# Own orders for the filling steps of a transformer block, with GpSimd's set-up work and the weight load split

## What is computed

```python
x = x + tanh(g_xattn) * xattn(layernorm(x), ctx)         # q from x, k and v from the context, softmax, Wo
x = x + tanh(g_ffn)  * block(layernorm(x))
# block: h = rms(x) * n1
#        q, k = rms per head of h @ wq.T, h @ wk.T; v = h @ wv.T; causal softmax; @ wo.T (first 32 columns zeroed)
#        xf = rms(x + ao) * n2;  gates = top 2 of softmax(xf @ gate_w.T), renormalised
#        o0, o2, o3: gelu networks;  o1: silu(..) * (..);  out = x + sum gates * o  (first 32 columns of the sum zeroed)
```

## Time and profile before

| | us |
|---|---|
| median of 3 runs | 1200.54 (1198.05 to 1200.64) |
| the profiled execution | 1201.37 |
| its span | 1199.6 |
| PE busy | 1030.4 (86%) |
| DVE busy | 828.7 (69%) |
| ACT busy | 740.2 (62%) |
| POOL busy | 346.7 (29%) |

### The profile page before, as it was taken

How to read it: one execution, slowest core, us unless ns; L and a number is a source line. 1 busy time by engine, 2 the same in 40 slices (tenths; PEclk the granted TensorE clock), 3 DMA queues, 4 the chain that set the end, 5 groups by cost and what they waited for, 6 DMA issues and landing times. The chain is left out here.

```text
span 1199.6 us, 26646 instructions
## 1 busy us (share of the span) xinstructions
PE 1030.4 (86%) x8578; PEld 623.6 (52%) x8578; DVE 828.7 (69%) x2264; ACT 740.2 (62%) x1329; POOL 346.7 (29%) x513
## 2 busy tenths in 40 slices
PE   2365779999999899999989899999989899988797
PEld 1133445555556555555556555555556555555454
DVE  6237577777787877777787877777787777764523
ACT  1144466766676676766676776766676776755343
POOL 4610323314141513314141513214131514213030
PEclk9576789999999999999999999999999999999799
DMA  4325343343444434243444434243444433221300
GB/s 155 54 70 136 101 118 102 96 111 71 114 118 115 118 96 107 83 112 67 114 118 115 118 102 106 85 106 67 114 117 115 118 106 102 86 43 53 63 10 10
DMA packets 78549, 114.28 MB, mean 95 GB/s; under 512 B 9136, under 2 KB 41520, under 8 KB 78384
## 3 DMA queue, kind: packets, MB, share of 16 engines
q1 hardware_dynamic: 78368, 111.58, 36.7%
q10 hardware_dynamic: 144, 2.21, 0.5%
HBM read 58.97 MB, written 53.74 MB: 94 GB/s over the span
## 5 line engine op out<-in xcount | busy, mean ns | idle before, releaser
L701 ACT ACTIVATE probs<-ps_s2a 120x512 f32<-120x512 f32 (+1 forms) x256 | 152.9, 597 | 81.1 <-PE ps_s2a L1056 72.7
L822 DVE TENSOR_REDUCE mpadA<-ps_w 128x4 f32<-128x480 f32 x256 | 150.4, 651 | 54.7 <-PE ps_w L1038 54.7
L822 DVE TENSOR_REDUCE mpadB<-ps_w 128x4 f32<-128x512 f32 x256 | 158.8, 683 | 29.1 <-PE ps_w L1038 29.1
L701 ACT ACTIVATE probs<-ps_s2b 120x512 f32<-120x512 f32 (+1 forms) x256 | 152.5, 596 | 0.0
L1103 PE MATMUL ps_w<-W,hid 128*128 128x96 f32 x1024 | 129.9, 281 | 15.1 <-ACT hid L697 10.9
L608 POOL TENSOR_SCALAR_AFFINE_SELECT probs<-probs 128x1024 f32<-128x1024 f32 x128 | 140.1, 1094 | 0.0
L1103 PEld LDWEIGHTS ps_w<-W,hid 128*128 128x128 f32 x1024 | 120.6, 194 | 36.2 <-issue 26.2
L574 POOL TENSOR_TENSOR rB<-veB,neg_half 128x4 f32<-128x4 f32 x16 | 16.1, 1008 | 400.9 <-DVE veB L725 400.9
L1121 PE MATMUL ps_w<-xfT,W 128*128 128x512 f32 x160 | 85.1, 621 | 0.0
L697 ACT ACTIVATE hid<-ps_s2a 128x512 f32<-128x512 f32 x80 | 47.8, 598 | 51.6 <-PE ps_s2a L1114 39.7
L1056 PE MATMUL ps_s2a<-qdA,kstA 128*120 128x512 f32 x128 | 69.4, 542 | 11.4 <-DMA qdA<-mTA 5.0
(11 more groups left out here) (184 smaller groups left out, 2119.6 us busy)
## 6 DMA issues: line engine op xcount, KB each, us to landing
scratch_Aq<-split_q SPq DMA_DIRECT2D x48, 256.0 KB, 2.4
qdA<-scratch_Aq SPq DMA_DIRECT2D x64, 192.0 KB
scratch_Bq<-split_q SPq DMA_DIRECT2D x48, 256.0 KB, 2.4
scratch_Bk<-split_k SPq DMA_DIRECT2D x48, 256.0 KB, 3.0
qdB<-scratch_Bq SPq DMA_DIRECT2D x64, 192.0 KB
kstB<-scratch_Bk SPq DMA_DIRECT2D x64, 192.0 KB
scratch_Ak<-split_k SPq DMA_DIRECT2D x48, 240.0 KB, 2.9
kstA<-scratch_Ak SPq DMA_DIRECT2D x64, 180.0 KB
```

The lines of the kernel that those rows point to most:

```text
L701: nc.scalar.activation(probs[0:k, slot_of(part, *index), :], bank[0:k, :], ACT.Exp, scale=SCALE if part == "A" else 1.0).then_inc(done, 1)
L822: nc.vector.tensor_reduce(mneg[OP[part]][:, :, c, b], bank[:, 0:HT * k].rearrange("p (h k) -> p h k", h=HT), AX.X, ALU.max, negate=True).t ...
```

## The change

1. The second and third filling steps get orders of their own (`second_group`, `third_group`); the first and fourth keep the table's. The order is now passed to each step, and banks are given out along the order of the step (`bank_of_each_use(order)`), no longer along the full table, so in all steps but the loop's some tiles have other banks.
2. In the second step the transposes of the next group's x come behind six tiles more. In the third one the first estimate of part A stands before the q/k matmuls; the split of part B's q and k stands before the norm of x; the second and third estimate of part B are later; the fourth comes behind the keys of part N, and the transposed maxima of part B are last.
3. POOL clears half of `qdA` behind the first power. It clears `qdB` and `kstB` in the second step, behind that norm's power, and does not wait for the first keys. DVE clears only the other half of `qdA`.
4. The load of x is issued before SP's wait for the keys.
5. The weights are loaded in two DMAs, the first with the 512 columns of the cross-attention.

```diff
+def second_group():
+    return (one("N", "load", 0, None)
+            + estimate("A", 0) + estimate("A", 1) + estimate("A", 2) + estimate("A", 3) + one("A", "mT")
+            + one("N", "stats", 0, None) + exact("A", 0, 0) + exact("A", 0, 2)
...
+def third_group():
+    return (one("N", "load", 0, None)
+            + estimate("A", 0) + one("B", "qk", 0) + one("B", "qk", 1) + one("B", "qk", 2) + one("B", "qk", 3)
...
+            + one("N", "q") + one("N", "v") + one("N", "k") + one("A", "norm", 0, None) + estimate("B", 3)
+            + one("A", "hT") + one("B", "mT"))
...
-RAMP = [(-1, "N"), (0, "NA"), (1, "NAB"), (2, "NABD")]
+RAMP = [(-1, "N", first_group()), (0, "NA", second_group()), (1, "NAB", third_group()), (2, "NABD", of_parts("NABD"))]
...
+                        sp.dma_start(xt[:], x[bass.ds(g * G, G), :, :].rearrange("b t d -> t b d")).then_inc(x_loaded, 16)
+                        if not st.first("N"):
 
                             sp.wait_ge(kd_ready["A"], g)
-                        sp.dma_start(xt[:], x[bass.ds(g * G, G), :, :].rearrange("b t d -> t b d")).then_inc(x_loaded, 16)
...
-                            sp.wait_ge(a_cleared, 1)
+                            sp.wait_ge(a_cleared, 2)
...
                         if st.first("N"):
 
-                            pool.wait_ge(kd_ready["A"], 1)
+                            pool.memset(qd["A"][:, HT // 2:HT].bitcast(F32), 0.0).then_inc(a_cleared, 1)
+                        elif st.parts == "NA":
+
                             pool.memset(qd["B"][:].bitcast(F32), 0.0)
                             pool.memset(kst["B"][:].bitcast(F32), 1.0).then_inc(b_cleared, 1)
...
-            act.dma_start(W[:], weights).then_inc(weights_loaded, 16)
+            act.dma_start(W[:, 0:ATTENTION], weights[:, 0:ATTENTION]).then_inc(weights_loaded, 16)
+            act.dma_start(W[:, ATTENTION:], weights[:, ATTENTION:]).then_inc(rest_loaded, 16)
...
-            nc.vector.memset(qd["A"][:].bitcast(F32), 0.0)
+            nc.vector.memset(qd["A"][:, 0:HT // 2].bitcast(F32), 0.0)
...
                     elif (part, work) == ("B", "qk"):
+                        if st.first("B") and index == 0:
+                            pe.wait_ge(rest_loaded, 16)
```

More of the change, by code:

```diff
@@ L165, in bank_of_each_use @@
+def bank_of_each_use(order):
     at, out = dict.fromkeys(RINGS, 0), {}
-    for part, work, index, ring in SCHEDULE:
+    for part, work, index, ring in order:
         if ring:
@@ L170, in bank_of_each_use, with uses_before, of_parts, __init__ @@
     return out
[L173 to L179, removed]
+def uses_before(order, key=None):
+    bank, n = bank_of_each_use(order), dict.fromkeys(BANKS, 0)
+    for part, work, index, ring in order:
         if (part, work, index) == key:
             break
[L182 to L184 removed]
+        if ring:
+            n[bank[part, work, index]] += 1
+    return n
+def of_parts(parts):
+    return [use for use in SCHEDULE if use[0] in parts]
 PARTS = "NABDM"
[L189 removed]
+RAMP = [(-1, "N", first_group()), (0, "NA", second_group()), (1, "NAB", third_group()), (2, "NABD", of_parts("NABD"))]
 LOOP = (3, NG - 1)
[L191 removed]
+TAIL = [(NG - 1, "ABDM", of_parts("ABDM")), (NG, "BDM", of_parts("BDM")), (NG + 1, "DM", of_parts("DM")), (NG + 2, "M", of_parts("M"))]
+assert all(sorted(map(str, order)) == sorted(map(str, of_parts(parts))) for _, parts, order in RAMP + TAIL)
 class Step:
[L197 to L201, removed]
+    def __init__(self, t, parts, order):
+        self.t, self.parts, self.bank = t, parts, bank_of_each_use(order)
+        self.works = [(p, w, i) for p, w, i, _ in order]
+        self.before = {k: uses_before(order, k)[self.bank[k]] for k in self.works if k in self.bank}
+        full = uses_before(SCHEDULE)
         self.base = dict.fromkeys(BANKS, 0)
[L203 removed]
+        for t0, _, o in RAMP + TAIL:
             if parts == PARTS or t0 >= t:
                 continue
[L206 removed]
+            for b, n in uses_before(o).items():
                 self.base[b] += n
         if parts == PARTS:
[L209 removed]
+            ramp = {b: sum(uses_before(o)[b] for _, _, o in RAMP) for b in BANKS}
             self.base = {b: t * full[b] + (ramp[b] - LOOP[0] * full[b]) for b in BANKS}
@@ L222, in fills @@
     def fills(self, *key):
-        return self.base[BANK[key]] + self.before[key] + 1
+        return self.base[self.bank[key]] + self.before[key] + 1
     def drains(self, sources, fill=None):
@@ L251, in run_steps @@
 def run_steps(engine, step):
-    for t, parts in RAMP:
-        step(Step(t, parts))
+    for t, parts, order in RAMP:
+        step(Step(t, parts, order))
     with engine.Fori(*LOOP) as t:
-        step(Step(t, PARTS))
-    for t, parts in TAIL:
-        step(Step(t, parts))
+        step(Step(t, PARTS, SCHEDULE))
+    for t, parts, order in TAIL:
+        step(Step(t, parts, order))
 def build(nc, x, ctxT, weights, vcols, rows, out):
@@ L388, in build @@
         CONSTANTS = 32
+        ATTENTION = sum(n for _, n in WCOLS[:4])
         block = ctx.enter_context(nc.Block())
@@ L702, in step @@
                                              scale=SCALE if part == "A" else 1.0).then_inc(done, 1)
-                    elif work == "pv" and key in BANK:
+                    elif work == "pv" and key in st.bank:
                         act.wait_ge(full, st.fills(*key))
@@ L826, in step @@
                         c = index[1]
-                        u = BANK["D", "fill", ("e1_w1", c)]
+                        u = st.bank["D", "fill", ("e1_w1", c)]
                         if c:
```

73 lines of the change are left out of this document (46 added, 27 removed).

## The result

| | before | after |
|---|---|---|
| median, us | 1200.64 (1198.05 to 1200.97, 7 runs) | 1207.65 (1204.35 to 1211.41, 7 runs) |
| the profiled execution, us | 1201.37 | 1211.41 |
| its span, us | 1199.6 | 1209.7 |
| PE, DVE busy, us | 1030.4, 828.7 | 1033.5, 838.1 |

The ratio is 1.0064, with a 95% interval of 1.0042 to 1.0085: 7 us slower, where no change was forecast, and outside the range.

What follows compares the result with a forecast made beforehand. PE is busy 65.1 of 70 us in the loop, so the worth lies before it, in the filling steps. Terms -12.4 - 1.8 - 0.5 - 0.4 + 15.0 = -0.1 us; forecast 1200.4 us, no change, range 1195.0 to 1205.0.

Steps and rivals of the forecast that it cites:

- up to the first scores of the second step: Set-up through PE's first scores: half the clear leaves DVE, so statistics start earlier; 2.3 us less.
- the second step's wait, with the clock: Early causal factors and x load remove PE's wait before the transposes, 9.1 us, and an earlier full clock gives 1.0.
- the third step up to its first scores: Part A's first estimate goes ahead of the q/k matmuls, into DVE's idle time; net 1.8 us less.
- from there to X: Up to the third step's last residual: one estimate of part B leaves this stretch, 0.5 us of PE less.
- X: The start of DVE's last residual in the third step; 127.65 before, predicted near 113.
- from X to the first scores of part B: End of the third step: late maxima queue behind stack loads, scores at about X + 25 for X + 10; 15.0 us lost.
- the fourth step: Orders unchanged and only bank names move, here and in the tail; 0, at most 0.5 us either way.
- the loop: Fewer waits need a computed value, 89 PE register instructions for 99; 0.4 us less over 12 steps.
- Set-up: Before the first transposes: statistics at 8.2, and GpSimd's half clear beside DVE's xn costs 0 to 0.7, taken as 0.
- The rival on record: End of third step: maxima wait as long as an x load, landing at X + 28; 1204.5 us, chance 0.19.
- the middle of three readings: End of third step: maxima land with the last stack data at X + 24.9; between losses of 10 and 18 us.
- a wait of PE left in the second step: Rival: xn comes after PE wants it, so 3 us of the 9.1 stay; 1203.5 us, chance 0.05.

Runs made afterwards that it cites:

- e3: The changed kernel, with SP issuing part B's four maxima DMAs behind the stores and ahead of the eight stack loads in the third step; 1199.30 us.
- e4: The changed kernel, with part B's four maxima DMAs in the third step issued from ScalarE's queue, behind its copy of the maxima; 1204.80 us.
- e2: The changed kernel, with each of GpSimd's two groups of clears waiting until DVE has finished that step's xn; 1203.97 us.
- e7: The changed kernel with the table's orders in the second and third step; GpSimd's placement, x load and weights as changed; 1198.29 us.
- t2: t1 with the first estimate of part A ahead of the q/k matmuls in the third step; 1187.74 us.
- e1: The changed kernel with the end of the third step in the old order, the maxima ahead of the stores and stack loads; 1191.47 us.
- e5: The changed kernel with both the old end of the third step (e1) and the clears waiting for the norm (e2); 1188.54 us.
- e7b: e7 with GpSimd's clears also waiting for the norm they ran beside, as in e2; 1189.38 us.
- t1: e7b with one wait more: GpSimd starts the causal factors only when DVE's kdA is done; 1188.90 us.
- t3: t1 with the weights loaded in one DMA; 1189.42 us.
- t4: t1 with DVE clearing all of qdA and GpSimd none of it; 1192.36 us.

## Why the prediction was wrong

| term, us | forecast | trace | off by |
|---|---|---|---|
| up to the first scores of the second step | -2.3 | +1.6 | +3.9 |
| the second step's wait, with the clock | -10.1 | -10.4 | -0.3 |
| the third step up to its first scores | -1.8 | -0.5 | +1.3 |
| from there to X | -0.5 | -0.6 | -0.1 |
| from X to the first scores of part B | +15.0 | +18.0 | +3.0 |
| the fourth step | 0 | -0.8 | -0.8 |
| the loop | -0.4 | -1.0 | -0.6 |
| sum | -0.1 | +6.3 | +6.4 |

Each entry of the trace is what the difference between the two profiled executions gains over that stretch. It comes from 44.01 for 42.38 at the first scores, 65.16 for 73.94 at the query matmul, 97.22 for 106.52 at the third step's scores, 117.75 for 127.65 at X, 145.72 for 137.66 at part B's scores, and the two pairs of the loop. What follows behind the loop (3.7 us in this pair of executions) is not in the table. The table has the scatter of one execution in it: e3 and e4, whose instructions are the same up to X, have -11.2 for the second step and -1.5 for the third step's start.

**Set-up, the step that failed.** "The nearest row for such company is xn beside a GpSimd copy of 512 columns, 1.83 us against 1.11 alone: it costs 0 to 0.7, and I take 0". It cost 3.0. The 0.7 of the row was taken for what such company costs at most, and it was a wait for one instruction to end. The row itself shows it, when its four instructions are told apart: one takes 1.06 us and the others 0.33, and the long one is there while GpSimd's copy runs.

```profile
104.33 1.04 POOL L570 TENSOR_TENSOR xc<-x,one 128x512 f32<-128x512 f32 x1
L754 DVE TENSOR_SCALAR xn<-xt,mvA,rsA x4: 333/335/1059, 104.4 to 105.9; 128x128 f32<-128x128 f32 x4
```

So an `xn` that starts behind a GpSimd instruction ends only behind it, and its price is the length of the other instruction, 3.51 us for half of `qdA`, and not a share of its own. The reason given for 0, that the transposes could lose it only once, is no reason: once is 3 us. e2 takes this away: `xn` is back at 1.11 us, and the medians give 3.7 us back. The same holds for "the big clears of qdB and kstB now run from 41, beside a DVE with nothing to do": DVE had `xn` to do, the very instruction on which the term rested. And the factors beside `kdA`, which the prediction had put early without naming what DVE does then, cost 1.6 us (2.66 for the 1.10 below, from the kernel before). Of the two together, 4.5 us, 3.9 reach the first scores.

```profile
23.48 1.10 DVE L740 TENSOR_SCALAR kdA<-kTbA,pick 128x480 bf16<-128x480 bf16 x4
```

The Trainium skill has the rule that would have said so: "SBUF — State Buffer", section "Who interferes with whom", states that DVE and GpSimd share a pair of ports as an exclusive lock, that whoever is first keeps it for the whole instruction and the other blocks, that a `tensor_scalar` can ask for it, if its operands meet conditions (SBUF to SBUF is one), and a `tensor_reduce` does not. The rows agree: `xn` and `kdA` are held, and the reductions of `mpadA` take 2.35 us beside the factors and without them, though these also read PSUM, so the rows don't tell which of the two spares them. In the second step the hold is longer than one instruction (last section). The prediction cited the skill on DMA queues and not here.

**The second step, right for a wrong reason.** The size was right within 0.3 (within 1.1 by e3 and e4), but "the transposes in it only change place" did not hold: by e7, in the old place 5.92 us of PE's wait would have stayed. Two errors of the prediction, `xn` ready at 42 and the place immaterial, did not meet because the change moved the transposes past the end of the hold, with nothing to spare. That the size came out is luck.

**The third step's start.** The term had 1.8 for the estimate and 0 for `hb` behind the keys' work, with "at most the 1.8 us of that work". The estimate's part was right: from the transposes of `hb` to the first scores it is 1.6 us less than before (73.91 to 97.22, and 81.57 to 106.52). The difference lies ahead of it: from the query matmul to these transposes it is 8.75 us for 7.63. What lengthens it in this execution is the clock: the two query matmuls take 1.91 us for 1.02, and DVE's low part of the keys starts 5.1 us behind them. In e2, with the same order, they are at the full level, the low part starts 4.0 us behind them, and the stretch is 7.75 us: the 0 was right there. GpSimd's `xb` holds one of DVE's two products in each of the three kernels, `kdA` here (1.92 us for 1.10), and `hb` before and in e2 (2.03 and 2.06 for 1.10). Alone, the early estimate is worth 1.1 us at X and next to nothing in the loop (t2).

**The end of the third step.** The rival on record gave X + 28 and a loss of 18, and that is what came, to 0.1 us. The forecast took the middle of three readings, that the maxima land with the stacks' data, X + 24.9. Two parts were short. The stack loads start at X + 14.2 for the X + 12.8 forecast, so the last of the maxima is issued at X + 19.6 and not near X + 18. And behind that it is 8.4 us to the scores, not the 7 that the middle reading left. The row that bears on a small DMA behind large ones was at hand, the x load behind stacks with 10.4 us. That the place decides was right: e1 takes 16 us off.

**The chances.** Slower had 0.24, in two mechanisms, at 4 and 3 us. The first, the late landing, came with its 3.0 us; the second, a wait of PE left in the second step, did not. What made the rest, a held `xn` and a held `kdA` in the set-up, stood in no rival. The late landing and these holds don't exclude each other but add up, and the range had room for one mechanism at a time.

**What is best.** e5, e7b, t1, t2 and t3 (1187.7 to 1189.4) are about 1% faster than the kernel before and can't be told apart. What they share: the early causal factors, half of the clear on GpSimd behind `xn` and not beside it, and the maxima ahead of the stores. GpSimd's new placement carries the gain, as far as the runs tell it from the early load of x, which all of them have; the orders of the steps don't.

## What to carry to other kernels

When work is moved to GpSimd, ask which DVE instruction starts while it runs, and price the meeting with what is left of the GpSimd instruction, and of one right behind it, not with a share; a wait that lets the short DVE instruction go first can be worth more than the move itself. A DMA on which the next step waits is priced by what is on the DMA engines when it is issued: issue it ahead of the bulk traffic, and don't expect another queue to save it. And where two edits are made together, look for one that only hides what the other causes: try each with the other undone.

## What the runs showed of the hardware

- The hold spans more than one GpSimd instruction. In the changed kernel DVE's first two of four `xn` instructions start at 43.21 and 43.47 and last until 51.9, behind both clears (6.93 us from 43.13, 1.81 from 49.99), though each alone takes 0.34 us; e7 shows the same with 9.23 us for the four. DVE did not get in between the two clears. The durations of the four are the shortest, the median and the longest, in ns:

```profile
L799 DVE TENSOR_SCALAR xn<-xt,mvA,rsA x4: 328/4404/8668, 43.2 to 52.1; 128x128 f32<-128x128 f32 x4
```

- One DVE operation that reads PSUM is not held: four reductions of `mpadA` take 2.35 us beside GpSimd's clear of `qdB` (before, at 28.23), beside its factors (after, at 27.57) and beside nothing (after, at 36.84).
- Four DMAs of 8 KB land in 1.9 us (median) when they are issued ahead of the stack loads, in 5.7 (3.6 to 7.8) from ScalarE's queue beside them, and in 8.3 (3.5 to 8.7) behind eight of them on SP's.
- From X to the first scores of part B the old order takes the same time wherever it starts, and with the early estimate or without: X + 10.0 before, and 10.1 in e5, e7b, t1 and t2. The exception is e1, X + 11.1, where the four DMAs took 2.4 us at the median for 1.9; why is open.
- 2.6 us of delay at the first scores of the second step became 5.2 us at its end (t4 against t1). PE's clock rose some 10 us later, at about 55.5 for 45.2, with the same work done in front of it at the half level. A warning on reading it: for the changed kernel the clock column has 1.00 from 12 to 60, where the same 32 matmuls take 1.91 us at 49.58 and 1.07 at 54.15. There the durations of equal matmuls tell the level, and the column doesn't.
